# Tokens stay on chip through layer 0's normalisation, and each group's down weights are turned when the group needs them

## The reference

```python
xn = _layernorm(x)
x = x + _L0_attn_ref(xn, ...) + _L0_ffn_ref(xn, W1, W2, W3)
xn = _layernorm(x)
x = x + _L1_attn_ref(xn, ...) + _L1_ffn_ref(xn, w_gate, w_up, w_down)

def _L0_attn_ref(x, ...):          # x here is the normalised n1
    xn = _layernorm(x, ln_gamma, ln_beta)
    h = _ssm_scan(einsum(xn, W_in) + b_in, sigmoid(decay_logit))
    x = x + einsum(h, W_out) + b_out + xn * D_skip
    hf = relu(einsum(_layernorm(x, ln_gamma, ln_beta), W_down) + b_down)
    return x + einsum(hf, W_up) + b_up

def _L0_ffn_ref(x, W1, W2, W3):
    hidden = silu(x @ W1.T) * (x @ W3.T)      # 2048 wide
    return fwht(hidden) @ W2.T                # Walsh-Hadamard transform, then down
```

## Time and profile before

| | us |
|---|---|
| Median of 3 runs (lowest to highest) | 1873.22 (1871.0 to 1873.24) |
| The profiled execution's own time | 1869.85 |
| Its span in the trace | 1868.1 |
| PE busy | 1723.7 |
| DVE, ACT, POOL busy | 1042.1, 735.8, 265.9 |

### The profile page before, as it was taken

How to read it: one execution, slowest core, us unless ns; L and a number is a source line. 1 busy time by engine, 2 the same in 40 slices (tenths; PEclk the granted TensorE clock), 3 DMA queues, 4 the chain that set the end, 5 groups by cost and what they waited for, 6 DMA issues and landing times. The chain is left out here.

```text
span 1868.1 us, 24728 instructions
## 1 busy us (share of the span) xinstructions
PE 1723.7 (92%) x8364; PEld 1381.7 (74%) x8364; DVE 1042.1 (56%) x1788; ACT 735.8 (39%) x1530; POOL 265.9 (14%) x224
## 2 busy tenths in 40 slices
PE   6899999999999769979999899958899999999997
PEld 4566877777788658867777777747678888888885
DVE  4221365454522443449999799956365647556554
ACT  4521211221111332239999899953221222212121
POOL 3000210310310021100000000018203203203200
PEclk9999999999999979989999999979899999999999
DMA  9830110110100017833444444335200001101011
GB/s 302 282 103 1 57 46 18 51 46 6 51 6 35 34 68 239 305 157 86 126 124 133 126 123 126 96 135 179 90 1 34 25 11 34 34 0 34 11 45 45
DMA packets 87689, 159.78 MB, mean 86 GB/s; under 512 B 8345, under 2 KB 39449, under 8 KB 85922
## 3 DMA queue, kind: packets, MB, share of 16 engines
q1 hardware_dynamic: 87586, 158.52, 26.7%
HBM read 105.01 MB, written 53.48 MB: 85 GB/s over the span
## 5 line engine op out<-in xcount | busy, mean ns | idle before, releaser
L1784 DVE TENSOR_TENSOR pt_lo<-p_turn,pt_hi 128x512 fp32r<-128x512 f32 (+3 forms) x384 | 201.2, 551 | 24.9 <-ACT pt_hi L1759 17.4
L1777 DVE TENSOR_REDUCE row_top<-p_score 128x1 f32<-128x128 f32 (+7 forms) x256 | 189.8, 751 | 21.1 <-PE p_score L1711 20.9
L1229 DVE TENSOR_TENSOR hid<-hid,p_up 128x512 f32<-128x512 f32 x64 | 44.0, 688 | 277.9 <-PE p_up L737 259.4
L1751 ACT ACTIVATE prob<-p_score,row_top 128x128 f32<-128x128 f32 (+7 forms) x256 | 189.6, 744 | 8.0 <-DVE row_top L1777 5.9
L1722 PE MATMUL p_turn<-ident,prob 128*128 128x128 f32 x1152 | 183.2, 278 | 3.9 <-DVE pt_lo L1784 3.6
L1759 ACT ACTIVATE pt_hi<-p_turn 128x512 fp32r<-128x512 f32 (+3 forms) x384 | 182.0, 493 | 12.0 <-PE p_turn L1722 8.2
L1737 PE MATMUL p_o<-pt_hi,v 128*128 128x512 f32 (+3 forms) x384 | 149.2, 396 | 3.8 <-ACT o_both L1767 3.1
L1722 PEld LDWEIGHTS p_turn<-ident,prob 128*128 128x128 f32 x1152 | 133.4, 143 | 17.7 <-DVE pt_lo L1784 4.4
L990 ACT ACTIVATE hid<-p_gate 128x512 f32<-128x512 f32 x64 | 38.2, 598 | 268.3 <-PE p_gate L737 268.3
L1709 PE MATMUL p_score<-stack 128*128 128x512 f32 (+3 forms) x384 | 129.6, 392 | 14.0 <-PEq L53 7.0
L294 DVE TENSOR_TENSOR ff_hid<-ff_hid,ff_p_up 128x512 f32<-128x512 f32 x64 | 43.9, 686 | 162.8 <-PE ff_p_up L183 160.9
(11 more groups left out here) (242 smaller groups left out, 3955.4 us busy)
## 6 DMA issues: line engine op xcount, KB each, us to landing
stack<-qk_parked SPq DMA_DIRECT2D x256, 128.0 KB, 3.7
qk_parked<-qk SPq DMA_DIRECT2D x16, 1024.0 KB, 3.9
raw<-in_wgu SPq DMA_DIRECT2D x32, 256.0 KB
v_parked<-v_out SPq DMA_DIRECT2D x16, 512.0 KB, 4.8
v<-v_parked SPq DMA_DIRECT2D x8, 1024.0 KB, 8.9
o_parked<-o_both SPq DMA_DIRECT2D x64, 128.0 KB
o<-o_parked SPq DMA_DIRECT2D x8, 1024.0 KB, 9.0
ff_raw_gu<-in_wgu SPq DMA_DIRECT2D x16, 512.0 KB, 3.7
```

What stands on the lines that cost most here:

```text
L1751: act.activation(prob[r // QB][:, h % 2, r % QB, 0:width_of(r)], p_score[:, r % 2, 0:width_of(r)], ACT.Exp, bias=top[:, r:r + 1], accum_ou ...
L1777: dve.tensor_reduce(top[:, r:r + 1], p_score[:, r % 2, 0:width_of(r)], AX_X, ALU.max, negate=True).then_inc(topped, 1)
L1784: dve.tensor_tensor(pt_lo[:, slot, c0:W], p_turn[:, (BL * h + j) % TB, c0:W], pt_hi[:, slot, c0:W].bitcast(F32), ALU.subtract).then_inc(sp ...
```

## The change

Tokens: ACT writes n1 of each quarter not to `res` but to a buffer that nothing uses yet (`n1_1` in unit 1's half of `h_hi`, `n1_0` in unit 1's half of `hid`, `n1_2` in `d_hi`, `n1_3` in `d_lo`). `store_n1` and `reload_x` go; `res` keeps x. The state-space part loads tokens of x, and a new ACT step, `tok_norm`, normalises them again, for which scale and shift are kept in `inv1` and `neg1`. The steps that first write to a borrowed buffer wait for the turns of its quarter. `norm_first(2)` now stands behind chunk 1 of unit 0, `norm_first(3)` behind chunk 2, the turns of quarters 2 and 3 in chunk 3 of unit 0 and chunk 0 of unit 1 (they were in unit 1, chunk 1, and unit 2, chunk 0).

Down weights: a slice is now four of W2's 16 interleaved row sets with all 512 columns, so that rows of 8 KB are loaded and of 2 KB stored. The eight pairs of the first product stay where they were. Its result stays in DRAM, and each of the 16 chunks is loaded to the ring as a raw item (12 items a group now, for group 0 too). The second product of a chunk is one matmul (`turn_down`, L649) to `p_out`, from which ACT rounds `d_hi` (`down_round`) and DVE takes `d_lo` (`down_rest`). A group's four stand in unit 4g + 1, one before each half of chunks 1 and 2. `load_half`, `store_slice`, `first_rest` and `split_d` go.

```diff
+        n1_at = [0, nc.sbuf_base + 4 * NC * W, 0, 0]
...
         def d_item(g, c):
-            return 12 * g + 4 + c
+            return 12 * g + 8 + c
...
+        def halves_before(u, c, j):
+            n = 2 * c + j + 1
+            return [divmod(n, 2)] if u == 0 and 2 <= n < 2 * SL else []
+
+        def downs_before(u, c, j):
+            return [(u // TT, 2 * c - 2 + j)] if u % TT == 1 and c in (1, 2) else []
...
-                sp.dma_start(rot[s][:], w2c[:, :, SW * s:SW * s + SW]).then_inc(slice_in[s], 16)
+                sp.dma_start(rot[s][:], w2c[:, SR * s:SR * s + SR]).then_inc(slice_in[s], 16)
...
+                    g, i = divmod(k - RING, 12)
+                    if i < 8:
+                        sp.wait_ge(raw_split, 8 * g + i + 1)
+                    else:
+                        sp.wait_ge(d_turned, NC * g + i - 8 + 1)
...
             sp.dma_start(logit[:], t["logit"]).then_inc(const_in, 16)
-            store_n1(1)
-            store_half(1)
-            load_half(1)
...
+            for s in range(1, SL):
+                store_half(s)
+            for s in range(SL):
+                sp.wait_ge(half_out[s], 16)
             for k in range(8, 8 + RING):
                 load_raw(k)
...
             for g in range(1, NG):
                 split_gu(g)
-                split_d(g)
...
+            def turn_down(g, c):
+                k = d_item(g, c)
+                landed(pe, k)
+                if c >= 2:
+                    pe.wait_ge(d_split, NC * g + c - 1)
+                elif g:
+                    pe.wait_ge(added, J * (TT * g - 1) + c + 3)
+                else:
+                    pe.wait_ge(rot_copied, NCH)
+                pe.matmul(p_out[:, c % 2], turn_w[:, 1], raw[:, k % RING], start=True, stop=True).then_inc(d_turned, 1)
...
+            def tok_norm(i):
+                act.wait_ge(tok_in[i % 2], 16 * (i // 2 + 1))
+                act.activation(tok[:, i % 2], tok[:, i % 2], ACT.Identity, bias=neg1[:, i:i + 1],
+                               scale=inv1[:, i:i + 1]).then_inc(tok_normed, 1)
...
+            def down_round(g, c):
+                act.wait_ge(d_turned, NC * g + c + 1)
+                if g == 0:
+                    act.wait_ge(turned, 3 * KD)
+                act.activation(d_hi[:, c], p_out[:, c % 2], ACT.Copy, scale=ROOT).then_inc(d_round, 1)
...
                     if u == 0 and c == 1:
                         x_round_quarter(1, 0)
                         root(3, slice(2 * Q, 4 * Q))
+                        norm_first(2)
                     if u == 0 and c == 2:
-                        norm(2, 0)
...
+                        norm_first(3)
                         x_round_quarter(2, 0)
...
+            def down_rest(g, c):
+                dve.wait_ge(d_round, NC * g + c + 1)
+                if g == 0:
+                    dve.wait_ge(turned, 4 * KD)
+                dve.scalar_tensor_tensor(d_lo[:, c], p_out[:, c % 2], ROOT, d_hi[:, c].bitcast(F32), ALU.mult,
+                                         ALU.subtract).then_inc(d_split, 1)
...
+                    for down in downs_before(u, c, 0) + downs_before(u, c, 1):
+                        down_rest(*down)
```

More of the change, by code:

```diff
@@ L346, in layer_zero @@
     SL = 4
-    SW = D // SL
+    SR = NCH // SL
     FIRST = 4
@@ L563, in _ @@
             sp.dma_start(tok[0:R + 1, 0], t["up_rows"]).then_inc(rows_in, 16)
-            for s in range(2):
-                sp.wait_ge(rot_out[s], 16)
+            load_raw(8 + RING)
+            for k in range(12, 12 + RING):
+                load_raw(k)
             sp.wait_ge(up_split, 1)
@@ L568, in _ @@
             load_tok(1)
-            for k in range(8 + RING, 19):
+            for k in range(12 + RING, 23):
                 load_raw(k)
@@ L572, in _ @@
                 load_tok(i)
-            for k in range(19, 23):
+            for k in range(23, 27):
                 load_raw(k)
@@ L576, in _ @@
                 load_tok(i)
-            for k in range(23, 31):
+            for k in range(27, 35):
                 load_raw(k)
@@ L580, in _ @@
                 load_tok(i)
-            for k in range(31, 35):
+            for k in range(35, 39):
                 load_raw(k)
@@ L584, in _ @@
                 load_tok(i)
-            for k in range(35, 44):
+            for k in range(39, 48):
                 load_raw(k)
@@ L909, in root, with norm_first, norm_last @@
                 act.activation(sd[:, a], var[:, a], ACT.Sqrt).then_inc(sd_done, 1)
-            def norm(q, last):
-                act.wait_ge(mean_neg, 3 + q + 1 if last else min(q, 2) + 1)
-                if last:
-                    act.wait_ge(res_out[q], 32)
+            def norm_first(q):
+                act.wait_ge(mean_neg, min(q, 2) + 1)
+                for j in range(Q):
+                    i = Q * q + j
+                    act.activation(n1[q][:, j], res[:, i], ACT.Identity, bias=neg1[:, i:i + 1],
+                                   scale=inv1[:, i:i + 1]).then_inc(n1_done, 1)
+            def norm_last(q):
+                act.wait_ge(mean_neg, 3 + q + 1)
+                act.wait_ge(res_out[q], 32)
                 for i in range(Q * q, Q * q + Q):
@@ L1052, in _ @@
                 hi(u, NC - 1)
+                if inside and not odd:
+                    tok_norm(Q * q + 2)
+                    tok_norm(Q * q + 3)
                 if u == UNITS - 2:
                     root(9, quarter(0))
-                    norm(0, 1)
+                    norm_last(0)
                 if u == UNITS - 1:
@@ L1253, in _ @@
             add_eps(quarter(0))
-            rsqrt(1, quarter(0), mean_neg)
+            rsqrt(1, quarter(0), mean_neg, inv1, neg1)
             x_rest(0, 0)
@@ L1257, in _ @@
             add_eps(quarter(1))
-            rsqrt(2, quarter(1), mean_neg)
+            rsqrt(2, quarter(1), mean_neg, inv1, neg1)
             for u in range(UNITS):
@@ L1292, in _ @@
                         x_rest(1, 0)
+                        rsqrt(3, slice(2 * Q, 4 * Q), mean_neg, inv1, neg1)
                     if u == 0 and c == 2:
-                        rsqrt(3, slice(2 * Q, 4 * Q), mean_neg)
-                    if u == 1 and c == 0:
                         x_rest(2, 0)
```

231 lines of the change are left out of this document (85 added, 146 removed).

## The result

The changed kernel is slower: 1885.43 us (1883.17 to 1892.22, 4 runs) beside 1872.96 (1871.0 to 1873.24) for the kernel before on the same chip, ratio 1.0075, 95% interval [1.0048, 1.0102]. That is 12.5 and 13.6 us; the forecast was 7.0. The time lies outside the forecast's own range (1877 to 1884, or 3.8 to 10.8 us) and inside the outer one (1871 to 1888). So the traces lie 22.3 us apart: 18.9 up to the next stage, and 3.4 behind it, where both kernels do the same. What lies behind that point takes 1177.5 to 1182.4 us in the fourteen traces of this case.

What follows compares the result with a forecast made beforehand. PE, busy 92% of the span, bounds the kernel. Head -18.9, turns +10.3, waits +11.3, clock +4.3 sum to +7.0 us: 1876.9 on the profiled execution, 1880.2 on the median's scale; own range 1877 to 1884, outer 1871 to 1888.

Steps and rivals of the forecast that it cites:

- The wait in unit 0: Head, unit 0: PE's wait for ACT's copies, now behind quarter 2's norms, grows from 2.8 to 7.1 us.
- those of L649: Second turns in units 1, 5, 9, 13: PE waits for DVE's d_lo, 2.3, 4.5, 4.5 and 2.3 us.
- the 12 turns: Units 5, 9, 13: turns moved out of the head come back uncovered on PE, 12 x 0.86 = 10.3 us.
- the waits of units 5, 9 and 13: Third turn of each waits for down_rest of the first: 4.5 + 4.5 + 2.3 = 11.3 us.
- Nothing: ACT's 16 tok_norm and 12 down_round, and SP held at weights with token loads behind, cost no time.
- the clock term: Low clock after new waits: 0.75 us each in units 1, 13, 1.4 each in 5, 9; 4.3 in all, bounds 0 to 6.8.
- Nothing moves but by 0.5 us at most: Head up to quarter 1's turn at 45.23 us: engine orders unchanged and no DMA waited for, so at most 0.5 us shift.
- 109 to 115: Sign for the head: unit 2's second half starts near 112 us, right if within 109 to 115.
- A: Waits of units 1, 5, 9, 13 and state_stack: clock gives back, not slower, 1872.5 us; chance alone 0.13.
- B: Weights' round trip through HBM ends last: store takes 9.4 us, not 5.1; +6 us, 1886; chance 0.15.
- C: Unit 0: quarter 2's norms do not hold PE, wait stays 2.8 us, 1875.9; chance alone 0.09.
- D: Borrowed buffers not idle: unit 1's first silu or d_hi waits for quarters' turns, a few us; chance 0.03.

Runs made afterwards that it cites:

- e10_before_filled: Kernel before, plus 8 matmuls with unread results in each of its four 2.2 us waits for state_stack; 1865.83 us, ratio 0.9963.
- e7_three_filled: Changed kernel with the three edits, plus 8 unread matmuls in each of the four 2.2 us state_stack waits; 1854.47 us, ratio 0.9898 to before.
- e6_filled_turns: Changed kernel, plus 7, 16, 16 and 7 unread matmuls while PE waits for d_lo in units 1, 5, 9, 13; 1876.70 us, ratio 1.0022 to before.
- e3_pool_waits: Changed kernel, with POOL waiting for DVE's two rsqrt chains before splitting raw items 0 and 4; 1885.62 us, ratio 1.0070 to before.
- after_again: The changed kernel once more, unedited, with more executions; 1886.53 us, ratio 1.0076 to before.
- three edits: Changed kernel with down_rest ahead of product, pair (2,1)'s copies ahead of quarter 2's norms, POOL behind two rsqrt chains; 1860.15 us, ratio 0.9941 to before.

## Why the prediction was right in sign and short in size

**Right: the structure.** The wait in unit 0 was forecast at 7.1 us (6.98), those of L649 at 4.5, 4.5, 2.3 and 2.3 with the matmul pace (4.32, 4.32, 2.14, 2.14 without); `feed` does stand ahead of `d_lo` in time. The `state_stack` waits stayed. The rests give the sizes. Free of low pieces the kernel before takes 555.5 (`e10_before_filled`) and the changed one, with the waits for `d_lo` gone as well, 566.0 (`e7_three_filled`): 10.5 us for the 12 turns (forecast 10.3). A low piece costs some 1.5 us (570.5 and 574.0 with three and five, against 566.0), so `e6_filled_turns` without its three would take 577.3: 11.3 us for the waits of units 5, 9 and 13 (forecast 11.3). "Nothing" was right for `tok_norm` and for the waits on weights, and for the DMA that went away but for what its earlier landing did to POOL.

**Wrong: the clock term.** The changed kernel's rest is 12.8 us above that 577.3, the one before has 3.0 above 555.5. The difference is 9.8 us where the prediction had 3.6 from unit 2 on. Two parts: a wait of 4.3 us was put at 1.4 us, "near one stretch", and has two pieces, of which 5.3 us lie behind it, about 2.6 us lost; and old waits of 2.2 us that went unpunished before were taken as staying so. One low stretch for every two short waits was a mean over one execution, and the prediction moved the waits without asking that mean again. By the rule of the Trainium skill that it had weighed and set below the trace ("TensorE: Matmul & The Clock Gate", HAM oscillation) each pass with a wait long enough pays; units 5, 9 and 13 agree with it, unit 1 (no low stretch behind 2.1 us) does not.

**Wrong: the head's start.** "Nothing moves but by 0.5 us at most" up to 45 us: that turn starts 5.8 us later, at 51.04, so the head gained 12.7, not 18.9, and ended at 117.93, past the 109 to 115 that were called right. The step looked only for what transfers let start sooner on PE; POOL starting sooner beside DVE's chain was not asked, nor that PE's turns, started sooner, would stand idle for ACT and find the clock low. Half wrong, then: in the executions of `e3_pool_waits` and `e6_filled_turns`, without a long `neg`, the head ends at 112.0 and 112.6, and the median of the times doesn't tell the two apart.

**The sum.** -12.7 + 10.5 + 11.3 + 9.8 = +18.9 from trace to trace up to the next stage, as the stage's end says (708.05 - 689.14). The prediction worked from the same trace of before, so its sum misses the traces by 11.9 us, 6.2 in the head and 5.5 in the clock. The medians say 12.5 to 13.6, since before's profiled execution had some three low pieces fewer than its usual one (see `e10_before_filled`). That the forecast lies nearer to the medians than to the traces is luck. The granted clocks on record show the clock's part without any trace: a median of 0.968 for the kernel before and 0.962 for `after_again`, six or seven low pieces.

**Rivals.** A, the clock gives back, is refuted; it took. B: no row has L649 waiting for the DMA; the last slice's store of 1 MB landed in 4.4 us. Size is the smaller part of that: in the traces' packet records one of 512 B took 27 ns (median) before and one of 2 KB 85 ns now, which makes an estimated 3.5 and 2.7 us for 1 MB on 16 engines, beside landings of 9.4 and 4.4. C: L638's wait was 7.0 us. D: no row of PE's waits names a borrowed buffer.

## What to carry to other kernels

When PE is the bound, put the release of a PSUM bank ahead of every chain on the releasing engine that nobody needs so soon: here the order of one line was worth 18 us, more than the whole change. Price a wait of PE as its length plus what the clock takes behind it, here about 1.5 us for a punished one of 2 us and 2.6 for one of 4, and count the old waits again, since shifting them changes which are punished. Unread matmuls in such waits are a cheap test of the second part, and here a gain.

## What the hardware showed unexpectedly

- A DVE instruction on 128x4 elements took 1.12 us instead of 0.16 while POOL ran a split of 1.27 us, and weights that land 2 us sooner were what brought the two together.
- Matmuls whose result nobody reads, in waits that were there anyway, made the kernel before faster by 6.9 us and the changed one with its three edits by 6 to 8.
- Single executions of one kernel differ by as much as a term of the sum: twelve of `e6_filled_turns` lie between 1870.9 and 1881.4 us, 23 of the kernel before between 1864.2 and 1874.8.
